# Two layers of attention and feed-forward on one core: the products with the values taken two quads at a time

## The reference, cut to what matters

```python
x: (16, 512, 128) f32            # 16 sequences, 16 heads of 8
x = x + attn0(layernorm(x))      # causal: softmax(q k^T / sqrt(8), masked) v, projected
x = x + moe(layernorm(x))        # 8 experts, best 2, 128 -> 512 -> 128, gelu
x = x + attn1(layernorm(x))      # not masked, no projection
x = x + ffn(layernorm(x))        # w_down(silu(gate) * up), operands rounded to blockwise fp4
# attention, for each of 16*16 heads:
w = softmax(einsum('bhnd,bhmd->bhnm', q, k) * D**-0.5)
attn = einsum('bhnm,bhmd->bhnd', w, v)
```

## Time and profile before

| | us |
|---|---|
| median of 3 runs | 2312.15 (2309.03 to 2314.53) |
| the profiled execution, its own time | 2317.76 |
| its span in the profile | 2316.0 |
| PE, DVE, ACT, POOL busy | 2038.6, 1621.9, 1390.4, 1063.4 |
| mean granted clock of TensorE | 0.952 of full speed |

### The profile page before, as it was taken

One profiled execution on the slowest core, in us unless ns is written; L12 is line 12 of the kernel. 1 busy time (PEld: TensorE's weight loads), 2 busy tenths in 40 slices (PEclk: granted clock), 3 DMA queues, 4 the chain that ended last, 5 costly groups with the idle time before them and its releaser, 6 DMA issues.

```text
span 2316.0 us, 45088 instructions
## 1 busy us (share of the span) xinstructions
PE 2038.6 (88%) x13603; PEld 1060.0 (46%) x13603; DVE 1621.9 (70%) x4772; ACT 1390.4 (60%) x3097; POOL 1063.4 (46%) x1777
## 2 busy tenths in 40 slices
PE   2999999999999939999649999999999999999984
PEld 1455455554554429999613333333333333333333
DVE  3888888887888633321137888888888888888854
ACT  0466666666666624444207777777777776777772
POOL 6433746537455250000265656555565655654222
PEclk8899999999999969999859999999999999999997
DMA  5232223223222024444322222121222212121100
GB/s 175 81 93 67 85 74 91 73 71 92 71 89 82 20 73 143 144 142 140 90 73 66 73 58 68 54 62 54 66 59 57 70 55 60 55 64 50 47 6 14
DMA packets 154335, 174.12 MB, mean 75 GB/s; under 512 B 38448, under 2 KB 122096, under 8 KB 153968
## 3 DMA queue, kind: packets, MB, share of 16 engines
q1 hardware_dynamic: 144464, 153.85, 22.6%
q0 software_dynamic: 8192, 16.79, 2.5%
q10 hardware_dynamic: 1440, 0.60, 0.1%
HBM read 120.30 MB, written 49.28 MB: 73 GB/s over the span
## 4 chain that ended last, share of the span: by engine, by line
PE 27%; DVE 12%; issue 5%; ACT 4%; POOL 2%; DMA 0%; SPq 0%; ACTq 0%; DVEq 0%; POOLq 0%
PE bank L1560 8%; PE bank L1538 6%; DVE l_rowmax L1770 6%; PE bank L1548 6%; ACT l_probs L1679 3%; DVE l_h L1790 1%; PE bank L1593 1%; PE bank L1574 1%; DVE l_hq L199 1%; PE bank L1631 1%; DVE l_hq L216 1%; DVE l_stats L1804 1%; DVE l_hq L222 1%; PE bank L1621 1%; PE bank L1579 1%
## 5 line engine op out<-in xcount | busy, mean ns | idle before, releaser
L1770 DVE TENSOR_REDUCE l_rowmax<-bank 128x1 f32<-128x512 f32 x1024 | 642.7, 682 | 109.6 <-PE bank L1538 109.4
L1679 ACT ACTIVATE l_probs<-bank 128x512 f32<-128x512 f32 x1024 | 549.1, 605 | 134.8 <-PE bank L1548 134.5
L865 DVE CUSTOM_DVE_ANT_0 bank<-bank,mask_rows_q 128x512 f32<-128x512 f32 (+3 forms) x1024 | 476.6, 518 | 101.9 <-PE bank L625 95.6
L781 ACT ACTIVATE l_probs<-bank 128x512 f32<-128x512 f32 (+3 forms) x1024 | 389.2, 443 | 150.0 <-PE bank L637 144.0
L1538 PE MATMUL bank<-k_stack,q_stack 96*128 96x512 bf16 x1024 | 395.0, 387 | 68.9 <-DVE l_rowmax L1770 43.9
L1548 PE MATMUL bank<-q_stack,k_stack 128*128 128x512 bf16 x1024 | 387.3, 382 | 1.6 <-ACT l_probs L1679 1.4
L625 PE MATMUL bank<-k_stack,q_stack 96*128 96x512 bf16 (+3 forms) x1024 | 316.8, 314 | 25.4 <-DVE l_rowmax L865 14.8
L635 PE MATMUL bank<-q_stack,k_stack 128*128 128x512 bf16 (+3 forms) x1024 | 307.6, 308 | 0.2
L1560 PE MATMUL bank<-l_probs,v_aug 128*32 128x512 f32 x2048 | 272.8, 605 | 29.4 <-ACT l_probs L1679 28.7
L637 PE MATMUL bank<-mask_rows_k,ident_bf 128*128 128x128 bf16 x1024 | 221.1, 221 | 0.0
L1174 ACT ACTIVATE experts_hT<-bank,experts_b 128x256 f32<-128x256 f32 x288 | 118.3, 471 | 158.2 <-PE bank L1136 158.2
(11 more groups left out here) (259 smaller groups left out, 3015.7 us busy)
## 6 DMA issues: line engine op xcount, KB each, us to landing
q_stack<-scratch SPq DMA_DIRECT2D x384, 96.0 KB
k_stack<-scratch SPq DMA_DIRECT2D x384, 96.0 KB
experts_w<-in_w SPq DMA_DIRECT2D x72, 256.0 KB, 2.4
scratch<-l_q_parts SPq DMA_DIRECT2D x32, 384.0 KB, 2.7
scratch<-l_k_parts SPq DMA_DIRECT2D x32, 384.0 KB, 3.0
experts_rows<-rows_in SPq DMA_DIRECT2D x72, 128.0 KB, 2.1
rows_out<-experts_y SPq DMA_DIRECT2D x72, 128.0 KB, 2.1
q_stack<-l_rowmaxT SPq DMA_DIRECT2D x384, 4.0 KB
```

What stands on the lines that cost most here:

```text
L781: nc.scalar.activation(probs[:, (a * HG + j) % PSLOTS, c0:S], bank[:, c0:S], ACT.Exp, scale=SCALE).then_inc(t_read, 1)
L865: nc.vector.tensor_tensor_reduce(scores, scores, m["mask_rows_q"][:, S - keys(t):S], 1.0, LOWEST, ALU.add, ALU.max, rowmax[:, g % 2, c:c + ...
L1679: nc.scalar.activation(probs[:, (a * HG + j) % PSLOTS, :], bank[:, :], ACT.Exp, scale=SCALE).then_inc(t_read, 1)
L1770: nc.vector.tensor_reduce(rowmax[:, g % 2, c:c + 1], bank[:, :], X_AXIS, ALU.max).then_inc(s_read, 1)
```

## The change

probs_v is called in every slot as before, but for a quad with an even number it does nothing, and for an odd one it does the quad before and then this one (quad_v, the old probs_v). `probs` grows from 8 to 12 slots, and exp of quad a waits for the product of quad a - 3 in place of a - 2. The 8 KB for each partition that this needs are found in two ways: b2 (4 KB) moves out of the memory that lives through layer_zero into that of experts, where SP loads it after the loads of tile 0, and DVE waits for it by a semaphore of its own at its start, while PE waits for w2 alone; and `passed` (2.3 KB, an intermediate of the routing) lies in slots 2 and 3 of `probs`. Nothing else in the order of any engine is touched.

```diff
-PSLOTS = 2 * HG
+PSLOTS = 3 * HG
...
-            b2 = dram["b2"]
-            sp.dma_start(m["b2"][:, :, :], bass.AP(b2.tensor, b2.offset, [[0, P], [E, NE], [1, E]])).then_inc(m["experts_loaded"], 16)
...
             def probs_v(a):
+                if a % 2 == 0:
+                    return
+                for quad_ in (a - 1, a):
+                    quad_v(quad_)
+
+            def quad_v(a):
                 b, quad = divmod(a, QUADS)
                 g, t = divmod(quad, TT)
                 pe.wait_ge(t_read, at[("exp", a, HG - 1)] + 1)
...
-                if a >= 2:
-                    act.wait_ge(pv_done, a - 1)
+                if a >= 3:
+                    act.wait_ge(pv_done, a - 2)
...
-            for j in range(3):
-                load(j)
+            load(0)
+            sp.dma_start(b2[:, :, :], bass.AP(dram["b2"].tensor, dram["b2"].offset, [[0, P], [E, NE], [1, E]])).then_inc(b2_loaded, 16)
+            load(1)
+            load(2)
...
-            dve.wait_ge(m["experts_loaded"], 32)
+            dve.wait_ge(b2_loaded, 16)
```

More of the change, by code:

```diff
@@ L388, in layer_zero @@
         count, tiles, ends = sb("count", [P, NE]), sb("tiles", [P, NE]), sb("ends", [P, NE])
-        by_expert, passed = sb("by_expert", [P, NE, NE]), sb("passed", [P, NJ, NE])
+        by_expert, passed = sb("by_expert", [P, NE, NE]), probs[:, 2:4, :].rearrange("p a n -> p (a n)")[:, 0:NJ * NE].rearrange("p (t e) -> p t e", e=NE)
         expert_f, start_f, row_f, end_f = sb("expert_f", [P, NJ]), sb("start_f", [P, NJ]), sb("row_f", [P, NJ]), sb("end_f", [P, NE])
@@ L1030, in _ @@
             after(nc.vector.tensor_reduce(ends[:, :], by_expert[:, :, :], X_AXIS, ALU.add))
-            after(nc.vector.tensor_tensor(passed[:, :, :], tile_no[:, :].unsqueeze(2).broadcast_to([P, NJ, NE]),
+            after(nc.vector.tensor_tensor(passed, tile_no[:, :].unsqueeze(2).broadcast_to([P, NJ, NE]),
                                           wide(ends[:, :], NJ), ALU.is_ge))
-            after(nc.vector.tensor_reduce(expert_f[:, :], passed[:, :, :], X_AXIS, ALU.add))
-            after(nc.vector.tensor_tensor(passed[:, :, :], passed[:, :, :], wide(tiles[:, :], NJ), ALU.mult))
-            after(nc.vector.tensor_reduce(start_f[:, :], passed[:, :, :], X_AXIS, ALU.add))
+            after(nc.vector.tensor_reduce(expert_f[:, :], passed, X_AXIS, ALU.add))
+            after(nc.vector.tensor_tensor(passed, passed, wide(tiles[:, :], NJ), ALU.mult))
+            after(nc.vector.tensor_reduce(start_f[:, :], passed, X_AXIS, ALU.add))
             after(nc.vector.tensor_tensor(row_f[:, :], tile_no[:, :], start_f[:, :], ALU.subtract))
@@ L1072, in experts @@
         y = [sb(f"y{k}", [P, SUB, E]) for k in range(LANES)]
+        b2 = sb("b2", [P, NE, E])
         w4 = sb("fp4_w", [P, len(weights4), HID])
@@ L1079, in experts @@
         h_mm, h_ready = sem("h_mm"), sem("h_ready")
-        y_mm, y_ready = sem("y_mm"), sem("y_ready")
+        y_mm, y_ready, b2_loaded = sem("y_mm"), sem("y_ready"), sem("b2_loaded")
         fp4_loaded, fp4_step, fp4_made = sem("fp4_loaded"), sem("fp4_step"), sem("fp4_made")
@@ L1120, in _ @@
         def _(pe):
-            pe.wait_ge(m["experts_loaded"], 32)
+            pe.wait_ge(m["experts_loaded"], 16)
             def turned_rows(j):
@@ L1221, in _ @@
                     nc.vector.tensor_tensor(y[j % LANES][:, :, :], y_bank[j % 2][:, 0:TILE].rearrange("p (s e) -> p s e", s=SUB),
-                                            m["b2"][:, e, :].unsqueeze(1).broadcast_to([P, SUB, E]), ALU.add).then_inc(y_ready, 1)
+                                            b2[:, e, :].unsqueeze(1).broadcast_to([P, SUB, E]), ALU.add).then_inc(y_ready, 1)
                     if 0 <= j - FIRST_PART < PARTS4 * len(weights4):
@@ L1888, in build @@
             m["w2"] = mem.sb("w2", [P, NE, FC, E])
-            m["b2"] = mem.sb("b2", [P, NE, E])
             load_constants(nc, m, dram, NB)
```

## The result

| | before | after |
|---|---|---|
| median, same chip | 2313.34 us (2309.03 to 2315.04) | 2386.41 us (2381.88 to 2390.57) |
| span of the profiled execution | 2316.0 us | 2388.8 us |
| mean granted clock | 0.952 | 0.947 |

What follows compares the result with a forecast made beforehand. PE with DVE close behind, each waiting for the other through three max-score banks, was taken as the bound. Layer_one +31, layer_zero +22 and b2's load +1 made +54 on 2312.15: 2366 us (2345 to 2398; stated range 2300 to 2400).

Steps and rivals of the forecast that it cites:

- The pace: Layer_one timings read before the change: product 0.31 us after the last max scores, DVE starting 0.42 after scores start.
- The drains: Changes of matmul form around PE's products: one entry and exit saved per two quads, 0.17 us a pair, 44 us.
- the gap: Time between max scores before and after a burst in layer_one: to grow by 0.92 us, from 1.54 to 2.46.
- Rival 3: At each double burst, the second quad pays its own drain, 0.08 us more: nothing saved, +20, 2386 us; chance 0.10.
- Layer_one: Stage term: +1.9 us for each of 14 feed-forward batches, +1.8 for each of the first two; +31 us, bounds -22 to +46.
- the walk: Step-by-step reckoning of PE, DVE and ACT from burst to burst; +1.9 us for a layer_one batch with feed-forward.
- Layer_zero: Stage term: +1.4 us a batch over 16 batches, +22 us, bounds -22 to +37.
- values and projection at two slots' ends give back 0.9: Layer_zero: this work at two slots' ends was to return 0.9 us of each batch's +1.3.
- The statistics: Layer_zero's layer norm statistics, 1.29 us of DVE in each of two legs that DVE now sets: cost 1.0 a batch.
- b2: Its new 512 KB load goes ahead of tile 1's rows on SP's queue in experts: +1 us, 0 to 3.
- Rival 1: Both layers: PE sets the time and only drains count, needing DVE below about 0.5 us a maximum; 2269 us, chance 0.20.
- Rival 2: The walk holds in one layer only; layer_zero's sum would be -22 to 0, total 2322 to 2344 us; chance 0.15.

Runs made afterwards that it cites:

- e2: The changed kernel with one product in each slot again in layer_zero alone, double bursts kept in layer_one: 2345.12 us, 1.0141 of the kernel before.
- e1: The changed kernel with one product in each slot again in both layers, keeping twelve slots and the moved b2 load: 2318.66 us, 1.0008 of the kernel before.
- e4: The changed kernel with each DVE row maximum over the first half of a bank: 2252.91 us, 0.9736 of the kernel before.
- e3: The kernel before with each DVE row maximum over the first half of a bank: 2229.41 us, 0.9645 of the kernel before.
- e8: The changed kernel with double bursts only in layer_one's slots 14, 0, 2 and 4, single ones elsewhere: 2369.35 us, 0.9934 of the kernel before.
- e9: The kernel before with four banks for max scores and three for exp scores, instead of three and four: 2325.36 us, ratio 0.9806.
- e11: The changed kernel with one product per slot and the slots' middle turnings moved into odd slots: 2355.76 us, 0.9932 of the kernel before.
- e12: The same kernel as e1, run on a slow chip: 2384.41 us, 0.9989 of the kernel before there.

## Why the prediction was right, and which of its terms were off

The forecast was 2366 us, slower, with a range to 2400; it came to 2386. Sign and mechanism held; the size fell 20 us short, and part of what closed the sum was luck, as said below.

**The pace** was as read: 0.31 before a burst, 0.42 to DVE's start. **The drains** were sized at 0.17 us a pair and measured 0.23 (1.09 less 0.86), so 59 us of saving rather than 44; **the gap** grew to 2.40 and not 2.46. Both were too pessimistic, and still the kernel is slower than forecast. Rival 3 named 2386, the very time that came, and is refuted by the same rows: the second quad's loads did not wait, the burst is 1.86 and not 2.00. The rule that it rested on, that weight loads overlap running matmuls only where the row group differs (the Trainium skill, TensorE: Matmul & The Clock Gate, Part 3, The mechanism), does not hold for these four-strip products.

**Layer_one**, stretch by stretch, from the first max scores behind one burst to those behind the next; the measured numbers are of batches without a fall of the clock:

| slots | predicted | measured |
|---|---|---|
| 14 to 0 and 0 to 2 | -0.3 | -0.31 |
| 2 to 4 | -1.0 | -0.30 |
| 4 to 6 | +0.9 | +0.12 |
| 6 to 8 | +0.9 | +0.83 |
| 8 to 10 | +0.5 | +0.42 |
| 10 to 12 | +0.9 | +0.85 |
| 12 to 14 | 0 | -0.02 |
| sum | +1.9 | +1.6 |

Five of seven lie within 0.1 us. The two that do not, 2 to 4 and 4 to 6, cancel (-0.1 forecast, -0.18 measured), which is luck. In 2 to 4 the longer burst did cover 0.85 of the 1.54 us in slot 4, as forecast, but a wait for DVE of 0.79 us came in slot 3, which had lost its product; the walk had no such wait. In 4 to 6 the product that left slot 5 was saved, where the walk gave nothing for it: the max scores go on at DVE's pace there, 0.60 us apart, with no longer wait. The first two batches came to +2.0 us together, for +3.6 forecast. The six falls of the clock then bring 10 us that no step of mine had, and the stage ends at +34, near the +31, but by 24 of mechanism and 10 of clock.

**Layer_zero is the mis-sized term**: +22 forecast, +35 by the stage, 40 by e2. The four slots that I walked from rows 7 came out well (8 to 12: predicted +0.32, measured +0.38). The step that failed is "values and projection at two slots' ends give back 0.9", and with it the walk of one kind of batch for all. Batches come in two kinds: every second one also carries the gate and the routing of two batches between slots 14 and 6, some 6 us more of PE and 6 of DVE. The table has the us that a batch without a fall of the clock got longer. The kernel before has no such batch of the second kind, so there e1 and e2 stand for it, which have its order in layer_zero:

| slots | without routing | with routing |
|---|---|---|
| 14 to 2 (values at the end of slot 1) | +0.3 | +1.1 |
| 2 to 6 (projection at the end of slot 5) | 0.0 | +1.2 |
| 6 to 10 (statistics in slots 6 and 7) | +0.6 | +0.6 |
| 10 to 14 (statistics in slot 13) | +0.8 | +0.8 |
| sum (forecast +1.4) | +1.7 | +3.7 |

With the credit, the two upper rows should have come to 2 x 0.32 - 0.9 = -0.3 together. They came to +0.3 in the one kind and +2.3 in the other. The statistics cost some 0.6 us above plain slots for the 1.0 that I had said, with the wait of 0.85 us where the product of slot 13 had been the cover. No row of layer_zero stood behind the credit, and the batches with routing were not walked; 16 batches at the mean of the two kinds are 43 us.

**b2** was estimated at 1 us (0 to 3). What lies between the layers grew by 2.8 us, and PE at the turning of tile 1's rows waited 4.01 us, before 2.03. But e1 and e2, which load b2 in the same place, wait 2.94 us there and need 400.3 and 397.8 us between the layers, against 399.8 before. So the wait is 1 to 2 us longer, as estimated, and no run shows that the whole got longer by it. The wait after the change:

```profile
904.53 0.69 PE L1135 MATMUL bank<-ident,experts_rows 128*128 128x128 f32 x2 [4.01 <-DMA experts_b<-in_b]
```

**What the profile after should have shown**: PE's wait for DVE grew as said, above all in slot 7. DVE's idle time before its maxima was to grow by more than half, and in the groups by line it fell (88.6 to 76.6). The idle time of a gap is booked on the first instruction of DVE behind it, and where PE turns the outputs that is the reciprocal (30.4 to 67.7 us in layer_one, and 1.50 us at 510.23 in layer_zero): I had named the wrong row.

**Rival 1** asked for maxima below 0.5 us. e4 has them at 0.42 and is 23.5 us slower than e3: its condition was not enough, since it looked at plain pairs and left out the slots in which DVE has long steps. Outside slots 6 to 8 next to nothing was lost with such maxima, but what the form changes save did not show there either. Rival 2 (one layer only) is out by e2: both layers cost.

## What to carry to other kernels

Work of PE that stands where PE would wait anyway is free; moved next to other work of the same kind it is paid in full, and the wait that it covered comes into view. So before instructions are bunched to save the changes between them, list for each place that loses its piece what that piece covered (here DVE's 2.7 us of fixed steps), and for each place that gets it how long the readers' banks last (here three banks of 0.6 us against a gap of 2.4). Bunch only where neither is hurt (e8), and try the split of the banks between the readers first: it was worth three times as much (1.9% in e9 for 0.7% in e8, each on a chip of the slow kind). And when a walk stands for all batches, look first whether they are of one kind.

## What the runs showed of the hardware

- Two quads of products with 32 columns of weights, in four strips that use all rows, run at 0.86 us for the second one: the weight loads (0.11 us each) are hidden under running matmuls, across the boundary of the quads too. A pair saves 0.23 us against two single bursts.
- In layer_one the waits of PE of 2.69 us in slot 7 were followed, in six of fourteen batches, by 3.4 us at the lower granted clock (0.51 and 0.53 in two such windows), with matmuls of 512 columns starting 0.43 us apart in place of 0.22. The six cost about 10 us, by batches that are 1.6 us longer.
- Double bursts are not needed for such falls, and no one length of the wait goes with them. With single bursts the kernel before had none in layer_one (wait of 1.66 us in slot 7), but ten in layer_zero; e1, whose layer_one has the same order, had three there (0.57 and 0.58), all within 2 us behind the wait of 1.54 us in slot 4; e11 had seven, six of them behind 1.7 us in slot 7 (0.50 in two such windows). e3, with 0.93 us in slot 7, had none. What decides in which batch the clock falls stays open.
- The same kernel took 2318.66 us on one chip (e1) and 2384.41 on another (e12). Its layer_one differed in two of eight stretches of a batch, slots 10 to 12 and 12 to 14, apart from falls of the clock. There DVE and ACT both took up scores about 1 us late (1.05 and 1.57 us idle at 1684.4 in e12). The cause was not found.
